# Direct products for the first three row tiles of a block-wise multiply, with its weight arithmetic on one engine

## The reference, cut to what matters

```python
# latents: layer-normed x, (8, 112, 1024); context: (8, 375, 1024)
kv = jnp.concatenate([context, latents], axis=1)
k = rms_norm((kv @ Wk).reshape(...))        # Wk: 1024 x 1024, 8 heads of 128
v = (kv @ Wv).reshape(...)
q = rms_norm((latents @ Wq).reshape(...))   # 32 heads
out = softmax(q k / sqrt(128)) v
x = x + tanh(g_xattn[0]) * (out @ Wo)
```

## Time and profile before

| what | value |
|---|---|
| median of 3 runs | 2744.36 us (2743.04 to 2744.92) |
| the profiled execution, its own time | 2745.68 us |
| its span, first to last instruction | 2743.9 us |
| mean granted TensorE clock | 0.986 |
| busy: TensorE, VectorE, ScalarE, GpSimd | 2649.5, 1468.9, 1255.8, 1013.0 us |
| moved by DMA | 304.91 MB, mean 111 GB/s |

### The profile page before, as it was taken

The page is one execution under the profiler, slowest core; times in us unless marked ns, Lnnn a source line. Parts: engine busy times, 40 slices in busy tenths (PEclk is TensorE's granted clock), DMA queues, the critical chain, the costliest instruction groups (busy, mean ns, idle before and its releaser), DMA issues. The chain is left out here.

```text
span 2743.9 us, 38502 instructions
## 1 busy us (share of the span) xinstructions
PE 2649.5 (97%) x13585; PEld 2262.4 (82%) x13585; DVE 1468.9 (54%) x2578; ACT 1255.8 (46%) x2754; POOL 1013.0 (37%) x857
## 2 busy tenths in 40 slices
PE   4999998999999999999999999989999999999998
PEld 3888777888888887788888888878999888788887
DVE  6666776444533335665665566536324001777776
ACT  5555664232433336655555455415224212655544
POOL 5455546545211114655555555402000000444430
PEclk8999999999999999999999999989999999999999
DMA  3566554232332334533333333232113223433311
GB/s 138 184 208 207 188 176 157 104 112 103 127 100 89 101 98 127 169 108 104 108 108 97 104 108 108 68 138 84 41 54 108 68 81 91 118 89 87 84 46 54
DMA packets 315029, 304.91 MB, mean 111 GB/s; under 512 B 125744, under 2 KB 253480, under 8 KB 314840
## 3 DMA queue, kind: packets, MB, share of 16 engines
q1 hardware_dynamic: 312728, 298.26, 35.5%
q10 hardware_dynamic: 2112, 4.19, 0.4%
HBM read 212.97 MB, written 89.41 MB: 110 GB/s over the span
## 5 line engine op out<-in xcount | busy, mean ns | idle before, releaser
L45 PE MATMUL pb<-p_ws,p_xs 128*128 128x512 f32 x872 | 350.5, 402 | 28.0 <-DVE p_xs L393 22.9
L47 PE MATMUL pb<-p_ws,p_xs 128*128 128x512 f32 x872 | 343.5, 394 | 0.0
L46 PE MATMUL pb<-p_ws,p_xs 128*128 128x512 f32 x872 | 343.2, 394 | 0.0
L1460 ACT ACTIVATE at_p<-pb,at_nmax 112x487 f32<-112x487 f32 x256 | 171.3, 671 | 315.2 <-DVE at_nmax L1536 315.2
L677 POOL TENSOR_TENSOR p_xr<-p_xf 128x512 f32<-128x512 f32 x152 | 216.7, 1441 | 173.1 <-ACT p_xf L814 131.0
L1298 POOL TENSOR_TENSOR at_k<-at_kr,at_k 128x488 fp32r<-128x488 f32 (+1 forms) x94 | 116.5, 1240 | 375.0 <-DVE at_k L1550 375.0
L992 DVE TENSOR_TENSOR p_c<-pb,p_c 128x512 f32<-128x512 f32 x246 | 161.0, 685 | 167.9 <-PE pb L47 167.0
L45 PEld LDWEIGHTS pb<-p_ws,p_xs 128*128 128x128 f32 x872 | 166.1, 190 | 63.6 <-DVE p_xs L393 24.8
L47 PEld LDWEIGHTS pb<-p_ws,p_xs 128*128 128x128 f32 x872 | 165.9, 190 | 36.0
L46 PEld LDWEIGHTS pb<-p_ws,p_xs 128*128 128x128 f32 x872 | 166.3, 191 | 32.8
L1555 DVE TENSOR_TENSOR at_ptlo<-pb,at_pthi 125x448 fp32r<-125x448 f32 (+1 forms) x256 | 147.9, 620 | 79.7 <-ACT at_pthi L1482 79.7
(11 more groups left out here) (262 smaller groups left out, 6839.3 us busy)
## 6 DMA issues: line engine op xcount, KB each, us to landing
p_raw<-in_L_xattn_Wq_dram SPq DMA_DIRECT2D x32, 512.0 KB, 4.2
at_raw<-in_L_xattn_Wo_dram SPq DMA_DIRECT2D x64, 256.0 KB, 2.7
xT_d<-p_xf SPq DMA_DIRECT2D x15, 1024.0 KB, 5.2
p_xf<-xT_d SPq DMA_DIRECT2D x15, 1024.0 KB, 4.9
qT_d<-p_qstage SPq DMA_DIRECT2D x56, 256.0 KB, 2.7
at_qr<-qT_d SPq DMA_DIRECT2D x64, 224.0 KB, 3.1
at_rb<-rT_d SPq DMA_DIRECT2D x64, 224.0 KB, 3.4
xc_raw<-xT_d SPq DMA_DIRECT2D x24, 512.0 KB, 4.1
```

The lines of the kernel that those rows point to most:

```text
L45: pe.matmul(out, stat_hi, mov_hi, start=start, stop=False)
L46: pe.matmul(out, stat_hi, mov_lo, start=False, stop=False)
L47: return pe.matmul(out, stat_lo, mov_hi, start=False, stop=stop)
L1460: act.activation(pr[:, p, h, 0:KVLEN], score_bank(m)[0:QLEN, 0:KVLEN], ACT.Exp, bias=nmax[:, p, h:h + 1], accum_out=rsum[:, p, h:h + 1]).t ...
```

## The change

1. **Direct products.** In the keys' pass tiles 0, 1 and 2 (p = 0 and p = 1) are multiplied by plain blocks: two steps for tile 0, four for the pair, each step two products into one quarter of the result. The values' pass keeps the scheme for all.
2. **Weights.** The four plain blocks are cast and their lows made first (jobs 0 to 3), each into the place of a product that they don't serve; the sums follow while the direct steps run, and sums 5 and 6, whose places are taken, are formed in place of blocks (0, 1) and (1, 0) and cast during pair 2 (jobs 4 to 8: 36 lows of slices in all, 28 before). All 20 sums and all lows of weights are VectorE's, in the values' pass too.
3. **Loads.** Each block is loaded in two halves; ScalarE issues (0, 0) and (1, 0), SP issues (0, 1) and (1, 1) between tiles 0 and 1 of x and ahead of the small loads. Block (0, 0) no longer lies in the result's buffer.
4. **Order.** New slots for p = 0 to 2; B starts one pair later (p = 2 to 12); tanh and the scaling of the queries' norm weight move from K(0, 1) to B(0).
5. **Attention.** The load of a tile of x stands at the end of SP's unit instead of its start.

```diff
-            quads = [cb[:, 1, :, :], at("p0_wb22", ...)[:], ...]
+            quads = [at("p0_wb11", [P, HK, CW], F32, R1 + 65536)[:], at("p0_wb22", ...)[:], ...]
...
+            def direct(w, p):
+                return w == 0 and p < 2
+
+            def steps(w, p):
+                if direct(w, p):
+                    return (2, 3, 0, 1) if p else (0, 1)
                 return range(NJ) if p else (1, 2, 3, 6)
...
+            def x_of(w, p, j):
+                if direct(w, p):
+                    return j // 2, j % 2
...
+            def lows_on_pool(w, p, j):
+                return j in (3, 4) and not direct(w, p)
...
+            def sets(w, p, j):
+                if direct(w, p):
+                    return [(j, 1.0)]
+                return {0: [(2, 1.0), (3, -1.0)], 1: [(1, 1.0), (0, -1.0)]}.get(j, [])
...
+            LATE = (("WS", 4), ("WS", 6), ("WS", 3), ("WS", 5))
...
-                    if 1 <= p <= 11:
-                        put(0, p, 5, "B", 2 * (p - 1))
-                        put(0, p, 6, "B", 2 * (p - 1) + 1)
-                for m, j in enumerate((0, 4, 5)):
+                    if 2 <= p <= 12:
+                        put(0, p, 5, "B", 2 * (p - 2))
+                        put(0, p, 6, "B", 2 * (p - 2) + 1)
+                for w, p, m, job in ((0, 1, 0, 4), (0, 1, 1, 5), (0, 2, 0, 6), (0, 2, 1, 7), (0, 2, 2, 8)):
                     for k in range(HK):
-                        put(0, 0, m, "WK", j, k)
-                put(0, 0, 1, "WS", W_ORDER[6])
+                        put(w, p, m, "WK", job, k)
+                for m, j in ((0, 2), (1, 4), (2, 6), (2, 3), (3, 5)):
+                    put(0, 0, m, "WS", j)
...
                 yield ("X", 0, 0)
                 yield ("X", 0, 1)
-                for m in range(4):
-                    j = W_ORDER[m]
...
+                for j in range(2):
                     yield ("XH", 0, 0, j)
                     yield ("XL", 0, 0, j)
+                for job in range(4):
+                    for k in range(HK):
+                        yield ("WK", job, k)
...
-            W_ORDER = (1, 2, 3, 6, 0, 4, 5)
-            W_DVE, W_POOL = (2, 5), (3, 6, 4)
+            W_SUMS = (2, 4, 6, 3, 5)
+            W_JOBS = ((0, quads[0]), (6, quads[3]), (5, quads[2]), (1, quads[1]), (2, wr[2][:, 1]), (3, wr[3][:, 1]), (4, wr[4][:, 1]),
+                      (5, quads[2]), (6, quads[3]))
...
                     load_x(0)
+                    for r, (h, c) in ((2, (0, 1)), (1, (1, 1))):
+                        for m in range(2):
+                            sp.dma_start(quads[r][:, 2 * m:2 * m + 2, :], block_of(wk0, h, c)[:, 2 * m:2 * m + 2, :]).then_inc(quad_loaded[r][m], 16)
                     load_x(1)
...
                     for e in order:
-                        if e[0] == "WS" and e[1] in W_POOL:
-                            sum_w(pool, w_sum_pool, e[1])
-                        elif e[0] == "XL" and e[3] in (3, 4):
+                        if e[0] == "XL" and lows_on_pool(*e[1:]):
                             low_x(pool, x_lo_pool, *e[1:])
...
-                        elif e[0] == "WV":
-                            j, m = e[1], V_ORDER.index(e[1])
-                            for k in range(1, HK, 2):
-                                pool.wait_ge(w_hi, N_WK + HK * m + k + 1)
-                                pool.tensor_tensor(ws[j][:, 1, k, :], raw_of(j, k), f32(ws[j][:, 0, k, :]), ALU.subtract).then_inc(w_lo_pool, 1)
...
                     def multiply(w, p, j):
+                        if direct(w, p):
+                            t, c = j // 2, j % 2
+                            if p and j < 2:
+                                pe.wait_ge(c_set, set_by[0, 0, j])
+                            for h in range(2):
+                                wait_x(pe, w, p, 2 * t + h)
+                                n = made[w, p, 2 * t + h]
+                                job = ((0, 2), (1, 3))[h][c]
+                                slot = W_JOBS[job][0]
+                                for k in range(HK):
+                                    if p == 0:
+                                        wait_low_w(pe, job, k)
+                                    last = product(pe, yb[j][:], xs[:, n % 10, 0, k, :], xs[:, n % 10, 1, k, :],
+                                                   ws[slot][:, 0, k, :], ws[slot][:, 1, k, :], h == 0 and k == 0, h == 1 and k == HK - 1)
+                            last.then_inc(y_done, 1)
+                            return
...
-                    for r, (h, c) in ((1, (1, 1)), (0, (0, 0)), (2, (0, 1)), (3, (1, 0))):
-                        act.dma_start(quads[r], block_of(wk0, h, c)).then_inc(quad_loaded[r], 16)
+                    for r, (h, c) in ((0, (0, 0)), (3, (1, 0))):
+                        for m in range(2):
+                            act.dma_start(quads[r][:, 2 * m:2 * m + 2, :], block_of(wk0, h, c)[:, 2 * m:2 * m + 2, :]).then_inc(quad_loaded[r][m], 16)
...
                         elif e[0] == "WV":
                             j, m = e[1], V_ORDER.index(e[1])
-                            for k in range(0, HK, 2):
+                            for k in range(HK):
                                 dve.wait_ge(w_hi, N_WK + HK * m + k + 1)
...
                 for u in range(U):
-                    if source is not None and 1 <= u <= TT:
-                        sp.dma_start(x_sb[:, u - 1, :], source[(u - 1) * P:u * P, :]).then_inc(x_loaded, 16)
...
                     fetch_sums(u)
+                    if source is not None and 1 <= u <= TT:
+                        sp.dma_start(x_sb[:, u - 1, :], source[(u - 1) * P:u * P, :]).then_inc(x_loaded, 16)
```

More of the change, by code:

```diff
@@ L270, in events @@
-                    if 1 <= p <= 11:
-                        put(0, p, 5, "B", 2 * (p - 1))
-                        put(0, p, 6, "B", 2 * (p - 1) + 1)
-                for m, j in enumerate((0, 4, 5)):
+                    if direct(0, p):
+                        for m, c in enumerate(steps(0, p)):
+                            n = m + 2 - p
+                            put(0, p, n, "N", p, c)
+                            put(0, p, n, "NS", p, c)
+                            put(0, p, n, "M", p, c)
+                            put(0, p, n, "MS", p, c)
+                            put(0, p, n + 2 + (m if p == 0 else 2), "K", p, c)
+                        continue
@@ L603, in _ @@
                             sp.dma_start(wr[j][:, 1, :, :], wsum_d[j].rearrange("k p n -> p k n")).then_inc(ws_loaded[j], 16)
-                        if e[0] == "XH" and e[1] == 1 and e[3] == steps(e[2])[0]:
+                        if e[0] == "XH" and e[1] == 1 and e[3] == steps(*e[1:3])[0]:
                             p = e[2]
@@ L834, in take @@
                     def take(w, p, j):
-                        if j >= 2:
+                        if not sets(w, p, j):
                             return
@@ L838, in take @@
                         past = previous(w, p, 2)
-                        for c, s in (((2, 1.0), (3, -1.0)) if j == 0 else ((1, 1.0), (0, -1.0))):
+                        for c, s in sets(w, p, j):
                             if past is not None:
@@ L983, in take @@
                     def take(w, p, j):
-                        if not adds(p, j):
+                        if not adds(w, p, j):
                             return
@@ L987, in take @@
                         dve.wait_ge(c_set, set_by[w, p, j])
-                        for m, c in enumerate(adds(p, j)):
-                            before = [jj for jj in steps(p) if jj < j and c in adds(p, jj)]
+                        for m, c in enumerate(adds(w, p, j)):
+                            before = [jj for jj in steps(w, p) if jj < j and c in adds(w, p, jj)]
                             if before:
```

209 lines of the change are left out of this document (105 added, 104 removed).

## The result

The changed kernel takes 2729.1 us (median; 2724.2 to 2730.35, 5 runs) against 2744.36: a ratio of 0.9938, interval 0.9924 to 0.9953. It is faster by 15 us, where the forecast was 34 and the range began at 17. The profiled execution took 2724.2 for a span of 2722.4; it is the fastest of the five, 4.9 under their median.

The account below looks back on a forecast made before the run. TensorE, busy for 97% of the span, was taken to bound the kernel, so gains lie where it idles or runs slow. 23 + 10 + 1 = 34 us (17 to 43) off 2745.7, less 1.3 to the median, gave 2710 (2701 to 2727).

Parts of the forecast that it names:

- (a): Opening, tile 0: after its transposes, copies, casts and a low, the first product starts near 10 us, not 17.06.
- (b): Opening, block loads: all blocks and tile 1 in at about 15.5 us; first direct step ends near 18.
- (c): Opening, tile 2: lands at about 21 us; TensorE idles 3 us, plus 1.2 us for a stretch at half clock.
- (d): Opening, from 21 us: the remaining transposes and direct steps end at 53.5 us.
- (e): Opening, pair 2's first product: waits for a low of x in VectorE's queue until 57 us, a hole of 3.5.
- (f): Opening, pair 2 to pair 4's transposes: 22.7 us plus 2.9 casts, 2.8 product, 0.6 clock; mark at 86, not 109.3.
- Term 2: Turn from keys' to values' pass: all 28 lows on VectorE at 0.62 us shrink the holes; 10 us, bounds 4 to 13.
- Term 3: Attention: loads of x tiles move by one unit, one tight unit less; 1 us gained, bounds -1 to 2.
- A: Opening: tile 2 and pair 2 take more back, Term 1 falls to 14 or less, 2716 to 2727 us; chance 0.22.
- term 1: Opening of the keys' pass: direct products of tiles 0 to 2 need no sums; 23 us gained, bounds 14 to 28.
- B: Turn of the passes: bound by the reloads, so Term 2 is 3 us and the time 2717; chance 0.12.
- C: VectorE beside GpSimd: waiting a whole GpSimd instruction, an operation costs 2.2 us; 2.7 us more, 2713; no chance of its own.

Follow-up runs that it names:

- e9_b_ten: The changed kernel with the background sums in pairs 2 to 10, four each in pairs 3 and 4, none in 11 or 12: 2726.0 us.
- e12_three: The changed kernel with small loads behind tile 2's load, background sums in pairs 2 to 10, values' weights in order 0,1,2,3,6,4,5: 2718.4 us.
- e4_small_last: The changed kernel with the five small loads issued behind tile 2's load and the store of the turned tile 0: 2722.3 us.
- e8_one_queue: The changed kernel with all four plain blocks of the keys' first weights issued from ScalarE's queue, none from SP's: 2727.1 us.
- e5_k_first: The changed kernel with the keys' copies in pair 2 ahead of the casts of weights in ScalarE's queue: 2731.8 us.
- e15_no_gpsimd_both: The changed kernel without GpSimd's sums of x for the keys' pair 2 and the values' pairs 1 and 2, result incomplete: 2714.2 us.

## Why the prediction was wrong

The direction held, and in the opening the mechanism too: its holes were the place, and 15 to 16 us came from there. At the turn the mechanism failed. By the steps:

- (a), (b): right. First product at 10.36 (near 10); the first direct step ran without a wait on a block and ended at 18.6 (18).
- (c): tile 2 at 21.87 (21), and the clock fell after its hole, as allowed for (8.0 us for a step of 6.4; I took 1.2). (d): the steps ended at 54.95 (53.5).
- (e): 59.1 instead of 57. Of the 2.1 us some 1.6 came from before: the lows of sum 2 ended at 40.0, not 38.4. The price of GpSimd's sums was nearly right: I had 4.8 for three scales (2.6, and 2.2 for the sums beside them); with their reciprocals they took 5.2 (the scales 1.58, 1.57 and 1.55), and the low 0.5 more than its 0.62. Without those sums the product starts at 56.05.
- (f) failed, by 5.3 of the 7.4 us at the mark: 29 us were forecast from pair 2's first product to the mark, 34.3 measured. I put 2.9 down for waits behind ScalarE's casts; the holes are 1.16, 2.71 and 0.65, 4.5 together, 1.6 more. And I put 0.6 down for the clock; the work between the holes took 29.8 us instead of the 25.5 at full clock, 4.3 more, of which 3.1 lie in the two products of 4.3 and 4.4 us. The lower bound held this, though by its own items (1.7 for the small loads, 8.4 for the 12 lows, at least 1.2 for the clock) it should have been 12, not 14, and the range should have begun at 15 us.
- Term 2 failed, and is the larger error: 10 forecast, 0.8 measured, below my bound of 4. The step is its sentence "All 28 on VectorE at 0.62 take 17.4 us". The price at 0.62 was read with GpSimd idle; I took the lows off GpSimd and so took GpSimd for idle, though the same paragraph had its sum of x start 4.4 us earlier, into these lows. The rows of the kernel before already held the dear case, at up to 1.60 each and not only the 1.30 that I quoted, beside the very sums of the earlier trace rows:

```profile
21.86 12.84 DVE L1064 TENSOR_TENSOR p_ws<-p_wr,p_ws 128x512 fp32r<-128x512 f32 x8 [1.84 <-ACT p_ws L936]
```

Measured: 2.48 for four alone, 4.09 and 6.77 beside GpSimd. With the sums left out the turn is 6.6 to 7.9 us shorter, and the forecast of 10 would have been near.

- "Background sums one pair later" at nothing: the pass is 1.7 to 1.9 us longer, and of that the hole of 1.5 in pair 12 is shown. It stands in all thirteen profiles that keep these sums there, and in none of the three that move them away; moving them opened other holes, so that only 1.2 came back (e9_b_ten), or nothing (e12_three).
- Term 3: 1 forecast, 0.5 to 0.9 seen in two profiles, not shown: the stretch scatters by 3, and the holes beside the loads did not shrink.
- Rivals: A had the place of the opening's loss (pair 2 took more back; term 1 was 15.9, A had 14 or less). B had term 2 at 3, nearest to the 0.8, but not its reason: neither TensorE nor ScalarE waited for a reload of the sums there. C: a VectorE operation beside GpSimd took up to 1.7, more than the 1.30 of the earlier trace rows. C's 2.2 took GpSimd's operation at 1.62, which is itself a price beside VectorE; alone it took 1.29, so waiting out a whole one would be 1.9. D and E were far off.

Open are the first attention units, and why the pass varied from 266.5 to 268.3 with the background sums unmoved. It does not follow the opening: it took 268.2 and 268.3 behind short ones (e4_small_last and e8_one_queue, with a granted clock of 0.96 in 320:365), but 268.0 behind the longest (e5_k_first) and 266.8 behind the shortest (e15_no_gpsimd_both).

## What to carry to other kernels

When work is moved off GpSimd, price what VectorE then does by what GpSimd *still* has to do in that stretch, not by an idle neighbour, and lay both queues on one time axis. A move that starts an engine earlier may bring it beside the work that it was to relieve. Where a queue has no gap, a different order within it gives back a part of a hole at best (here 3.1 us of 7.3, then nothing) and moves the rest. Small loads ahead of a large one that TensorE waits for cost twice: here 3.3 us of its arrival, and 1.6 more through the clock.

## What the runs showed of the hardware

- A 128x512 operation of VectorE beside GpSimd's sums of x took 1.0 to 1.7 us (four in 4.09, 6.77, 6.82, 6.84) against 0.62 alone, and GpSimd's sum 1.3 alone, up to 2.2 beside it (five in 11.10). Where both ran back to back, each took the same time per operation: 1.60 and 1.62 in the kernel before (eight in 12.84 and 12.95), 1.69 and 1.69 at the turn (four in 6.77, two in 3.38). That is less than 0.62 and 1.29 in turn, 1.91. But which of the two gives way varied: four lows took 2.48 inside those 11.10. What decides it was not tried. Scales of 128x512 went from 0.69 to 1.55 and more; additions that read PSUM (0.69) hardly changed.
- The clock: behind the hole of 3.2 us before tile 2 the step took 8.0 us with a granted clock of 0.91 in 20:40, part of it at 1.2 GHz; behind holes of 0.3 and 2.3 us there (e4_small_last, e15_no_gpsimd_both) it took 6.4. Yet in pair 2 a hole of 2.71 was followed by a product of 4.4 us instead of 2.8, so the length of one hole does not tell.
- Five small loads ahead of tile 2 cost 3.3 us of its arrival (21.87 against 18.54).
- ScalarE issues transfers at the price of its own work: with eight instead of four ahead of its first copy, the copy started 2.6 us later (8.87 against 6.32).
